# A 16-iteration DVE program rolled into a loop, an empty outer loop on PE removed, and two DVE steps moved

## The reference, cut to what matters

```python
def _derivative(q, p, drive, coupling, bias):
    i_couple = jnp.tanh(q) @ coupling.T
    dq = q - q ** 3 / 3.0 - p + drive + i_couple + bias
    dp = EPSILON * (q + ALPHA - BETA * p)
    return (dq, dp)

def _rk4_step(q, p, drive, coupling, bias):
    dq1, dp1 = _derivative(q, p, drive, coupling, bias)
    dq2, dp2 = _derivative(q + 0.5 * DT * dq1, p + 0.5 * DT * dp1, drive, coupling, bias)
    dq3, dp3 = _derivative(q + 0.5 * DT * dq2, p + 0.5 * DT * dp2, drive, coupling, bias)
    dq4, dp4 = _derivative(q + DT * dq3, p + DT * dp3, drive, coupling, bias)
    ...                       # weighted sum, clipped to +-20

# the network, on each state q
g = _qlinear(qx, sx, sc, w_gate, ...)      # 512 -> 1408, inputs rounded to fp8
u = _qlinear(qx, sx, sc, w_up, ...)
t = silu(g) * u                            # rounded to fp8 again
y = _qlinear(qt, st, sct, w_down, ...)     # 1408 -> 512
x = x + y
```

## Time and profile before

| | |
|---|---|
| three executions | 1591.96, 1595.45, 1597.55 us |
| the profiled execution | 1595.45 us, of which its span is 1593.6 us and 1.85 us lie around it |
| PE busy | 1495.5 us (94%) |
| DVE busy | 1067.9 us (67%) |
| ACT busy | 589.5 us (37%) |
| POOL busy | 475.9 us (30%) |
| mean granted TensorE clock | 0.98 of full speed |

### The profile page before, as it was taken

The page is one execution under the profiler, slowest core; times in us unless marked ns, Lnnn a source line. Parts: engine busy times, 40 slices in busy tenths (PEclk is TensorE's granted clock), DMA queues, the critical chain, the costliest instruction groups (busy, mean ns, idle before and its releaser), DMA issues.

```text
span 1593.6 us, 45904 instructions
## 1 busy us (share of the span) xinstructions
PE 1495.5 (94%) x16619; PEld 933.2 (59%) x16660; DVE 1067.9 (67%) x3437; ACT 589.5 (37%) x1902; POOL 475.9 (30%) x673
## 2 busy tenths in 40 slices
PE   5999999998799999999999998989999999999994
PEld 1333333335675758576766754666666666666662
DVE  1676666775754545564556441578999999899986
ACT  2444444552011020202020102455655656665552
POOL 0212211211220202020211200235656655556650
PEclk9999999998989999999999999999999999999997
DMA  8111122214200000001010105011111111111111
GB/s 310 42 51 48 46 51 59 67 48 162 15 1 7 20 14 13 26 0 26 0 26 0 27 7 216 22 33 29 38 33 36 38 50 38 35 35 36 33 45 40
DMA packets 90922, 72.68 MB, mean 46 GB/s; under 512 B 32608, under 2 KB 82784, under 8 KB 89696
## 3 DMA queue, kind: packets, MB, share of 16 engines
q1 hardware_dynamic: 71056, 59.09, 12.5%
q10 hardware_dynamic: 18032, 6.88, 1.7%
q0 software_dynamic: 1760, 5.77, 1.3%
HBM read 54.77 MB, written 16.94 MB: 45 GB/s over the span
## 4 chain that ended last, share of the span: by engine, by line
PE 70%; DVE 18%; issue 4%; ACT 4%; DMA 1%; POOL 1%; DVEq 0%; SPq 0%; POOLq 0%; ACTq 0%
PE ps L720 14%; PE ps L710 12%; PE ps L638 11%; PE ps L650 11%; PE ps L828 9%; PE ps L755 3%; DVE mem L1373 3%; PE ps L779 3%; DVE mem L1424 3%; ACT mem L1067 2%; DVE ps L1400 1%; PE ps L844 1%; PE ps L805 1%; DVE mem L1556 1%; DVE mem L1414 1%
## 5 line engine op out<-in xcount | busy, mean ns | idle before, releaser
L828 PE MATMUL ps<-mem 128*32 128x128 f32 x8192 | 279.4, 277 | 36.3 <-ACT mem L1067 25.9
L828 PEld LDWEIGHTS ps<-mem 128*32 128x32 f32 x8192 | 211.6, 110 | 108.8 <-ACT mem L1067 70.0
L555 POOL TENSOR_TENSOR mem<-mem 128x256 f32<-128x256 f32 x128 | 93.0, 727 | 452.6 <-DVE mem L1284 452.6
L720 PE MATMUL ps<-mem 128*128 128x256 f32 x1024 | 222.3, 379 | 0.0
L720 PEld LDWEIGHTS ps<-mem 128*128 128x128 f32 x1024 | 193.9, 190 | 26.0
L710 PE MATMUL ps<-mem 128*128 128x512 f32 x448 | 196.7, 592 | 0.0
L638 PE MATMUL ps<-mem 128*32 128x384 f32 x2048 | 180.4, 494 | 9.6 <-DMA mem<-in_W_ih 5.7
L650 PE MATMUL ps<-mem 128*32 128x384 f32 x2048 | 178.9, 490 | 2.4 <-DVE mem L1204 2.4
L1027 ACT ACTIVATE mem<-mem 128x512 f32<-128x512 f32 x32 | 19.7, 630 | 386.8 <-DVE mem L1316 386.8
L1067 ACT ACTIVATE mem<-mem 128x64 f32<-128x64 f32 x512 | 109.8, 250 | 92.2 <-DVE mem L1373 86.4
L710 PEld LDWEIGHTS ps<-mem 128*128 128x128 f32 x448 | 83.6, 190 | 94.6 <-issue 94.2
(11 more groups left out here) (146 smaller groups left out, 2124.1 us busy)
## 6 DMA issues: line engine op xcount, KB each, us to landing
mem<-x_scr SPq DMA_DIRECT2D x128, 64.0 KB, 1.8
mem<-in_xT SPq DMA_DIRECT2D x64, 64.0 KB
mem<-in_Wq SPq DMA_DIRECT2D x1, 4096.0 KB, 12.5
mem<-in_Wo SPq DMA_DIRECT2D x1, 4096.0 KB, 15.0
q_scr<-mem SPq DMA_DIRECT2D x64, 64.0 KB, 1.6
mem<-q_scr SPq DMA_DIRECT2D x64, 64.0 KB, 1.9
out<-mem SPq DMA_DIRECT2D x64, 64.0 KB, 1.6
mem<-in_x SPq DMA_DIRECT2D x14, 256.0 KB, 2.7
```

Source lines behind the costliest of these rows:

```text
L555: pool.tensor_tensor(one, one, turned[h % 2].rearrange("p (b t) -> p b t", t=T), ALU.add).then_inc(qr_done, 1)
L720: mm = pe.matmul(ps[:, h % Q_BANKS, 0:BLK], wq[:, c, h * DH:(h + 1) * DH], xnb[:, c, :], start=(c == 0), stop=(c == NC - 1))
L828: mm = pe.matmul(ps[32 * j:32 * j + 32, st % 2, 0:P], thT[:, c, :], ct[:, c, j * P:(j + 1) * P], start=False, stop=(c == NC - 1), skip_gro ...
```

## The change

On DVE the groups 3 to 14 become a `Fori` loop like on the other engines. As a group's number is then a register, the count of `rk_v` at the start of a group is computed from it with the constant `GROUP_STEPS` = 15. Two things move so that a group looks the same in each pass: `t_bits` of the first part goes from slot 9 to slot 8, and that of the second part from slot 11 to slot 9, ahead of the first `t_grid`; the copy `tsy` goes from slot 15 to slot 5 of the next group. On PE the loop of a single pass is removed. ACT, POOL and SP have the same instructions as before.

```diff
+GROUP_STEPS = 15
...
-def in_groups(eng, group, loop=True):
+def in_groups(eng, group):
...
-    if loop:
-        with eng.Fori(LEAD, NTILE - 1) as g:
-            group(g, True, tiles(g))
-    else:
-        for g in range(LEAD, NTILE - 1):
-            group(g, True, tiles(g))
+    with eng.Fori(LEAD, NTILE - 1) as g:
+        group(g, True, tiles(g))
...
-                        stage(4 * g + k // 4 + (nought if isinstance(g, int) else 0), k // 4, k % 4)
+                        stage(4 * g + k // 4, k // 4, k % 4)
...
-            with pe.Fori(0, 1) as nought:
-                in_groups(pe, group)
+            in_groups(pe, group)
...
+                if tile(2) is not None and k == 5:
+                    wait_if(dve, f_ysc, tile(2))
+                    v.did(dve.tensor_copy(tsy, tsx))
...
+                    if k == 8:
+                        t_bits(v, i, 0)
                     if k == 9:
-                        t_bits(v, i, 0)
+                        t_bits(v, i, 1)
                         t_grid(v, 0)
                     if k == 10:
                         t_added(v, 0)
                     if k == 11:
-                        t_bits(v, i, 1)
                         t_grid(v, 1)
...
-                if tile(1) is not None and k == 15:
-                    if i is not None:
-                        dve.wait_ge(f_ysc, i + 1)
-                    v.did(dve.tensor_copy(tsy, tsx))
...
-                v = Steps(dve, rk_v, counts.get("next", 0))
-                if g == 1:
+                if not isinstance(g, int):
+                    base = counts["lead"] + (g - LEAD) * GROUP_STEPS
+                else:
+                    base = counts.get("next", 0)
+                v = Steps(dve, rk_v, base)
...
-            in_groups(dve, group, loop=False)
+            in_groups(dve, group)
```

More of the change, by code:

```diff
@@ L1561, in group @@
             def group(g, rk, tile):
-                v = Steps(dve, rk_v, counts.get("next", 0))
-                if g == 1:
+                if not isinstance(g, int):
[3 more added lines that the diff above has]
+                v = Steps(dve, rk_v, base)
+                if isinstance(g, int) and g == 1:
                     dve.wait_ge(ffn_ld, 16 * 6)
@@ L1566, in group @@
                     if rk:
-                        stage(g, k // 4, k % 4, g == NTILE - 1, lambda: slot(v, k, tile, rk))
+                        stage(g, k // 4, k % 4, isinstance(g, int) and g == NTILE - 1, lambda: slot(v, k, tile, rk))
                     else:
                         slot(v, k, tile, rk)
-                    if (g, k) == (1, 5):
+                    if isinstance(g, int) and (g, k) == (1, 5):
                         last_residual(1)
-                counts["next"] = counts.get("next", 0) + v.n
-            in_groups(dve, group, loop=False)
+                if isinstance(g, int):
+                    counts["next"] = counts.get("next", 0) + v.n
+                    if g == LEAD - 1:
+                        counts["lead"] = counts["next"]
+                else:
+                    assert v.n == GROUP_STEPS, v.n
+                    counts["next"] += (NTILE - 1 - LEAD) * GROUP_STEPS
+            in_groups(dve, group)
 def kernel(**inputs):
```

## The result

The changed kernel takes 1605.02 us in the median of nine executions (1600.04 to 1607.4), the kernel before 1595.45 us, run in turn with it. The ratio is 1.0058, with a 95% interval of 1.0044 to 1.0074: slower by some 9.3 us. The forecast was 1596.7 us with a range up to 1604, so the time lies 1 us outside the range: no change was foretold, and there is a loss.

A forecast was written before the change was run, and what follows sets the result against it. PE waits for the state of the stage before, a 2.13 us cycle; terms 0 + 1.4 + 0 + 0.4 - 0.4 - 0.35 + 0.3 - 0.1 = +1.25 us on 1595.45 give 1596.7 us, range 1591 to 1604 us.

The forecast's parts named there:

- slot 8: DVE's 640-column bits take 0.49 us, mostly in idle time; L1414 0.05 us late; cost 0, at worst +0.6 us.
- the pause that goes: DVE's idle time ahead of L1424, stage 7 of group 3, shrinks as the loop replaces plain code: -0.35 us.
- the seam: DVE's loop branch and register instructions at 12 group borders, before L1548: 0.12 us each, +1.4 us, at most 4.4.
- Slot 11: DVE's L1522 leaves this slot, freeing more than the 0.03 us its stage is over 2.13: -0.4 us.
- The end: Last group but one: DVE waits about 0.3 us for L1088's second part, +0.3; the group before saves 0.1 us.
- PE's loop: Removing PE's single-pass loop drops a branch and two or three instructions: 0, bounds 0 and -0.4 us.
- Slot 9: Bits of 768 columns replace those of 640; L1528 ends 0.06 us later, L1424 0.04 us late: +0.4 us.
- Register instructions: The 44 in DVE's loop body cost 0; upper bound 4.4 us, on 48 places ahead of L1398.
- first rival: Register instructions around the transposes, L1398 and L1414, and the unhidden seam cost time: 1604.1 us; chance 0.12.
- The second rival: DVE's loop body doesn't stay on chip; each of 11 branches back costs 1.8 us: 1616.5 us; chance 0.03.
- the third: DVE's loop form is faster, 0.06 us in 192 stages: 1585.2 us; chance 0.07, shared with more pauses gone.
- any stage that grew by over 0.1 us away from the border: Sign in the changed kernel's trace, away from the border of two groups, that would prove the accounting wrong.

The follow-up runs named there:

- run 1: Changed kernel with both exponent-bit operations back in slots 9 and 11, DVE's loop and the copy as changed: ratio to before 1.0010, 1597.07 us.
- run 2: Kernel before, DVE's groups written out, with only the two exponent-bit operations moved to slots 8 and 9: ratio 1.0034, 1602.5 us.
- run 5: Changed kernel with slot 8's bits cut in two, 320 columns staying and 320 going to slot 9: one execution, 1605.0 us.
- run 6: Changed kernel with POOL's addition of slot 7 cut from 512 to 64 columns: one execution, 1613.28 us.
- run 3: Kernel before with DVE in its loop and PE's one-pass loop gone, bits and copy where they stood: ratio 1.0014, 1598.22 us.
- run 4: Changed kernel with six met waits (three instructions) ahead of DVE's outer loop: ratio to before 1.0046, 1601.73 us.
- run 7: Changed kernel with DVE's code moved by 17 and by 18 instructions through met waits: one execution each, 1603.52 and 1606.34 us.
- e9: DVE's loop, bits in slots 9 and 11, six met waits ahead, start value written before slot work; against the kernel before: ratio 0.9989.
- e10: The same kernel as e9 run again against the kernel before: ratio 0.9998 (0.9984 to 1.0012).

## Why the prediction was wrong, step by step

**The step that failed is slot 8.** The forecast put the bits of 640 columns there at 0.49 us, 0.41 of them in DVE's idle 0.29, "L1414 starts 0.05 us late", and took 0, at worst +0.6 us. Measured: the instruction takes 1.00 us, L1410 is 0.56 us later in the stage than its pair before (2.05 us behind L1420, 1.49 before), and stages 8 and 9 give 12 x 0.545 = 6.5 us. Runs 1 and 2 show the edit's share, 5 and 6 the mechanism. The rest of the step stands: at 0.49 us the operation would have cost nothing, as forecast (run 6). The duration was taken from the slot that the operation came from, and nobody asked what POOL does in the slot that it went to. The rows had it: L1528 on 768 columns took 0.81 us, on 640 columns 0.63, and 128 columns more cost 0.06 us for the bits (0.55 to 0.49). The missing 0.12 us was POOL: its gate operation ended 0.39 us behind the start of the first and 0.28 us behind that of the second, and DVE's ended 0.42 and 0.35 us after it.

**The second step that failed is the pause that goes.** The copy in slot 5 cost 0 as forecast, and stage 5 still cost 1.8 us. The forecast had a term for DVE's program, a pause that goes (-0.35 us), and let it happen in the loop "in the first pass at most". It happens in every pass, 0.35 us in the first and 0.11 us in the eleven after it, and the change put it in front of an instruction that nothing hides (runs 3, 4 and 7). Stage 7 of group 3 has 0.41 us of idle time and no longer 0.76, but stage 5 of the same group has the 0.35 us in its place: the pause moved by two stages and nothing was gained. That the instructions have to be brought in, as the forecast put it, is shown by no run.

```profile
1111.04 0.30 DVE L1420 SCALAR_TENSOR_TENSOR ps<-ps,mem 128x128 f32<-128x128 f32 x1 [0.41 <-PE ps L825]
```

**Right in kind and size:** the seam, forecast 12 x 0.12, measured 12 x 0.13 = 1.6 us, at the place and on the way foretold. Slot 11, forecast -0.4, measured 12 x -0.031 = -0.37 us; with L1522 gone L1420 waits for PE again, and L1524 itself, now off POOL's gate operation, takes 0.55 and not 0.81 us. The end: forecast 0.3 us of waiting,

```profile
1580.68 0.56 DVE L1518 TENSOR_SCALAR mem<-mem 128x768 uint32<-128x768 uint32 x1 [0.33 <-ACT mem L1084]
```

measured 0.33. From L1522 at 1576.17 to the last copy of DVE (before 1583.02, after 1579.86 to 1587.00) it is 0.29 us longer. In sum the forecast had +0.2, and group 15 is 0.07 us longer and all that follows it 0.53; but the same kernel took 45.40 us there in e9 and 45.94 in e10, so the rest can't be told from scatter. PE's loop: 0, and nothing is seen of it.

**Slot 9**, forecast +0.4 us, can't be read in the changed kernel, where stage 9 starts late. By its rows DVE alone would have ended it after 2.16 us (L1524 ends 2.24 us behind L1420, less the 0.08 us by which L1424 starts ahead of L1528's end in slot 11). That is 0.03 us over the 2.13 before, an estimate of +0.3 us, but the stage took 2.225 us for the reason given above, and no run has slot 9 alone. **Register instructions**: the middle stages 2, 3, 6 and 10 are 2.13 us as before, and the four places ahead of L1394 show in stages 12 and 13 at most, 0.019 us each (of which stage 12 has 0.013 in run 2 too, without a loop), against which stage 14 gives 0.024. From the first transpose to L1394 it is 0.178 us in the mean over the loop, as to L1398 before. The forecast's 0 holds and its first rival, 1604.1 us, came near the time for a wrong reason: run 3 has its whole loop and costs 0.14%. The second rival (instructions fetched again, 1.8 us a pass) and the third (a faster form) are both out by the stages' times. The forecast had named what would prove it wrong, "any stage that grew by over 0.1 us away from the border", and stages 8 and 5 did. Over the twelve groups the parts are 6.5 us for stages 8 and 9, 1.8 for stage 5, 1.6 for the seam and twice -0.4 for stages 7 and 11, in sum 9.1 us beside the 9.0 measured.

## What to carry to other kernels

A duration belongs to the place where it was read: before an operation is moved, look at what the other of DVE and POOL does at the new place, since in these runs DVE's `tensor_scalar` from SBUF to SBUF and POOL's additions waited for each other's whole instruction. Compute the time of every stage from the start of one instruction that occurs once in each, and compare stage by stage; that told three causes apart in one table where the busy times hadn't moved at all. And making the other engine's instruction shorter doesn't end the wait if the next one in its queue moves up into the gap, as in run 6.

## What the runs showed that I had not expected

- DVE's `tensor_scalar` on float32 or uint32 in SBUF ends 0.35 us behind the end of POOL's instruction at 640 columns, 0.18 us at 320, however long it had waited (0.69, 1.00, 1.48 and 0.83 us); alone it takes 0.49 and 0.32 us. At 768 columns it is 0.42 us and 0.55 alone, so in each width some 0.14 us of its time passes while it is held. Operations of DVE that read PSUM took the same beside POOL as alone (0.29, 0.58 us).
- DVE pauses at two places 128 instructions apart in its program, for 0.35 us in the first pass of a loop and 0.11 us in each later one, seen here where the next instruction follows a wait that ends last. Three instructions more ahead of the loop take it away (stage 5: 2.285 to 2.154 us), eighteen bring it back elsewhere (stage 15: 2.120 to 2.260 us). Both times the profile named PE as the releaser.
